# Two banks for the score matmuls of the maxima and three for those of the keys, instead of three and two

## The reference

```
x = x + attn_a(layernorm(x));  x = x + ffn(layernorm(x))
x = x + attn_b(layernorm(x));  x = x + ffn(layernorm(x))
attn:  softmax(q k^T / 4) v, per head, then a projection       (attn_b: causal, rotated q and k)
ffn:   gate = sigmoid(x Wq^T routers^T); leaf_prob = products of g or 1-g along 8 levels (256 leaves)
       leaf_prob @ leaf_values, then a projection
```

## Time and profile before

| | us |
|---|---|
| median of three runs (1170.36 to 1172.85) | 1172.26 |
| the profiled execution, its own time | 1170.09 |
| its span, from the first to the last instruction | 1168.4 |

### The profile page before, as it was taken

The page is one execution under the profiler, slowest core; times in us unless marked ns, Lnnn a source line. Parts: engine busy times, 40 slices in busy tenths (PEclk is TensorE's granted clock), DMA queues, the critical chain, the costliest instruction groups (busy, mean ns, idle before and its releaser), DMA issues.

```text
span 1168.4 us, 18914 instructions
## 1 busy us (share of the span) xinstructions
PE 1085.8 (93%) x6160; PEld 544.6 (47%) x6160; DVE 894.7 (77%) x2494; ACT 752.7 (64%) x1549; POOL 307.6 (26%) x339
## 2 busy tenths in 40 slices
PE   5789999999999999999999999999999899998986
PEld 2223354444455545454455544455444455544544
DVE  3578788786977988788976979788886878877834
ACT  3067766766777667765787567775776665666562
POOL 3012101111403151131503233041513526262210
PEclk9589999999999999999999999999999998999989
DMA  7323130600406023051314213150321313022001
GB/s 206 79 73 73 46 83 19 144 19 20 126 19 145 20 65 100 19 127 37 107 39 110 55 38 109 37 127 19 94 70 37 109 38 117 28 83 64 20 19 36
DMA packets 77921, 81.09 MB, mean 69 GB/s; under 512 B 12640, under 2 KB 65280, under 8 KB 77824
## 3 DMA queue, kind: packets, MB, share of 16 engines
q1 hardware_dynamic: 77760, 79.86, 25.5%
q0 software_dynamic: 64, 0.03, 0.0%
HBM read 20.84 MB, written 8.39 MB: 25 GB/s over the span
## 4 chain that ended last, share of the span: by engine, by line
PE 64%; DVE 21%; ACT 5%; issue 3%; SPq 3%; DMA 2%; POOL 2%; DVEq 0%; POOLq 0%; ACTq 0%
PE ps_work L1232 14%; PE ps_out L1141 13%; PE ps_max L1095 12%; PE ps_key L1117 11%; PE ps_work L1260 9%; DVE neg_max L859 7%; PE ps_work L1197 3%; DVE scratch L1009 3%; ACT probs L743 2%; DVE scratch L1012 2%; DVE ps_max L855 2%; DVE scratch L1039 2%; PE ps_work L1151 1%; SPq L500 1%; DMA q_stack<-q_part 1%
## 5 line engine op out<-in xcount | busy, mean ns | idle before, releaser
L743 ACT ACTIVATE probs<-ps_key 128x512 f32<-128x512 f32 (+3 forms) x1024 | 515.8, 520 | 340.9 <-PE ps_key L1117 336.0
L859 DVE TENSOR_REDUCE neg_max<-ps_max 128x1 bf16<-128x512 f32 x512 | 336.6, 685 | 87.0 <-PE ps_max L1095 85.6
L1095 PE MATMUL ps_max<-k_stack,q_stack 96*128 96x512 bf16 (+3 forms) x1024 | 355.9, 352 | 34.8 <-DVE neg_max L859 15.2
L1117 PE MATMUL ps_key<-q_stack,k_stack 97*128 97x512 bf16 (+3 forms) x1024 | 348.7, 344 | 19.2 <-ACT probs L743 13.1
L855 DVE CUSTOM_DVE_ANT_0 ps_max<-ps_max,mask_b 128x128 f32<-128x128 f32 (+3 forms) x512 | 247.0, 503 | 105.0 <-PE ps_max L1095 103.0
L1095 PEld LDWEIGHTS ps_max<-k_stack,q_stack 96*128 96x128 bf16 x1024 | 99.6, 97 | 292.7 <-DVE neg_max L859 115.0
L1141 PE MATMUL ps_out<-probs,v_ones 128*32 128x512 f32 (+3 forms) x2048 | 233.8, 529 | 0.6 <-POOL probs L638 0.6
L638 POOL TENSOR_SCALAR_AFFINE_SELECT probs<-probs 128x512 f32<-128x512 f32 x128 | 82.2, 643 | 400.5 <-ACT probs L743 400.0
L1117 PEld LDWEIGHTS ps_key<-q_stack,k_stack 97*128 97x128 bf16 x1024 | 100.9, 99 | 144.1 <-ACT probs L743 90.7
L1141 PEld LDWEIGHTS ps_out<-probs,v_ones 128*32 128x32 f32 x2048 | 40.4, 108 | 73.6 <-issue 63.2
L855 DVE DVE_READ_ACCUMULATOR2_ANT neg_max<- 128x1 bf16 x512 | 72.6, 142 | 0.0
(11 more groups left out here) (90 smaller groups left out, 1257.0 us busy)
## 6 DMA issues: line engine op xcount, KB each, us to landing
k_stack<-k_part SPq DMA_DIRECT2D x48, 256.0 KB
q_stack<-q_part SPq DMA_DIRECT2D x48, 256.0 KB
k_stack<-k_part SPq DMA_DIRECT2D x96, 128.0 KB
q_stack<-q_part SPq DMA_DIRECT2D x96, 128.0 KB
x_in<-in_x SPq DMA_DIRECT2D x8, 512.0 KB, 4.0
q_stack<-shift_rows SPq DMA_DIRECT2D x256, 1.0 KB, 1.7
x_again<-in_x SPq DMA_DIRECT2D x8, 512.0 KB, 4.1
spill<-x_plain SPq DMA_DIRECT2D x8, 512.0 KB, 2.9
```

The lines of the kernel that those rows point to most:

```text
L743: act.activation(probs[step % RING][:, j, q0:T], ps_key[slot % 2][:, 0:T - q0], ACT.Exp, scale=SCALE).then_inc(on["exp_done"], 1)
L859: dve.tensor_reduce(out=dst, in_=src, axis=AX_X, op=ALU.max, negate=True)\
L1095: pe.matmul(dst[:, 0:keys], q_stack[n % 2][0:SPLIT_ROWS, h, P * qt:P * qt + P], k_stack[n % 2][0:SPLIT_ROWS, h, 0:keys], start=True, stop= ...
L1117: pe.matmul(ps_key[slot % 2][:, 0:T - q0], k_stack[n % 2][0:STACK_ROWS, h, P * kb:P * kb + P], q_stack[n % 2][0:STACK_ROWS, h, q0:T], star ...
```

## The change

The number of score banks goes from three to two, that of key banks from two to three. A unit's bank is now its number, counted through all phases, modulo two, so a score matmul always waits for the maximum two units back. A slot's key bank is its number, counted through all phases, modulo three, on TensorE and on ScalarE, and a key matmul waits for the exponential three slots back.

```diff
-SCORE_BANKS = 3
+SCORE_BANKS = 2
+KEY_BANKS = 3
 def score_bank(n, unit):
-    return (unit + n % 2) % SCORE_BANKS
+    return (n * SLOTS + unit) % SCORE_BANKS
         ps_max = [bank(f"ps_max{i}", [P, T]) for i in range(SCORE_BANKS)]
-        ps_key = [bank(f"ps_key{i}", [P, T]) for i in range(2)]
+        ps_key = [bank(f"ps_key{i}", [P, T]) for i in range(KEY_BANKS)]
...
                 act.wait_ge(on["keyed_full"], count.next("keyed_full"))
-                act.activation(probs[step % RING][:, j, q0:T], ps_key[slot % 2][:, 0:T - q0], ACT.Exp,
+                act.activation(probs[step % RING][:, j, q0:T], ps_key[(n * SLOTS + slot) % KEY_BANKS][:, 0:T - q0], ACT.Exp,
                                scale=SCALE).then_inc(on["exp_done"], 1)
...
-                if count.some("exp_done", 1):
-                    pe.wait_ge(on["exp_done"], count.of("exp_done", 1))
+                if count.some("exp_done", KEY_BANKS - 1):
+                    pe.wait_ge(on["exp_done"], count.of("exp_done", KEY_BANKS - 1))
                 count.add("exp_done")
                 h = GROUP * g + j
-                pe.matmul(ps_key[slot % 2][:, 0:T - q0], k_stack[n % 2][0:STACK_ROWS, h, P * kb:P * kb + P],
+                pe.matmul(ps_key[(n * SLOTS + slot) % KEY_BANKS][:, 0:T - q0], k_stack[n % 2][0:STACK_ROWS, h, P * kb:P * kb + P],
                           q_stack[n % 2][0:STACK_ROWS, h, q0:T], start=True, stop=True).then_inc(on["keyed_full"], 1)
```

## The result

The changed kernel takes 1223.3 us (median of four runs, 1216.0 to 1227.7) against 1172.6 before: 1.0425 times as long, 95% interval 1.0401 to 1.0449 (the two medians alone give 1.043). Forecast were 1203 us, with a range to 1217. The direction was right, the size was not: 51 us and not 31.

What follows compares the result with a forecast made beforehand. TensorE's own work was taken to set most of the time, then VectorE's maxima. Score-bank losses of 34.3 us less 3.3 gained by the key bank gave 31.0 us, so 1203 us, 2.6% slower, range 1184 to 1217.

Steps and rivals of the forecast that it cites:

- The step that VectorE's queue runs dry and TensorE's lumps come out behind: Units 7 to 16 and 43 to 58 of each phase: two banks hold TensorE one unit earlier; 3.5 us per plain phase.
- the busy times of all engines should stay: All engines, whole run: no instruction, transfer or engine changes, so busy times stay and the other edits cost nothing.
- four plain phases (5, 7, 9, 11): Plain phases between causal ones: 1.1 + 0.9 + 1.5 = 3.5 us late each, 14.0 us together.
- four causal ones (4, 6, 8, 10): Causal phases between plain ones: shorter maxima, 0.9 and 0.8 us late in two places, 1.7 each, 6.8 together.
- phases 12 to 14: Last three full phases, causal with extra VectorE rotations: 0.9 and 2.0 us late, 2.9 each, 8.6 together.
- phases 2 and 3: Third phase +0.3 us after its key matmuls give 0.8 back; fourth phase, plain, 3.3 us.
- phase 15 and the end: The last phase was put at 1.3 us longer.
- phases 0 and 1: First two phases: third key bank removes 3.9 us in 6 waits and some 0.9; VectorE costs 1.5 back: -3.3 us.
- the opening loop: Opening, only score matmuls and maxima: two banks lose nothing, 0.48 us per refill against 0.60 us per maximum.
- the 0.06 and 0.42 us: Opening estimate: 0.06 us from a maximum's end to the waiting score matmul, 0.42 us more until its maximum can start.
- Buffering doesn't matter: Rival, TensorE's waits for VectorE: a bank only moves the waiting, only the key side counts; -13.1 us, 1159; chance 0.05.
- The delays add up: Rival, score-side delays: no give-back by idle time, +44 us or more, 1216 to 1225; chance 0.14 (over 1212).

Runs made afterwards that it cites:

- the run with long fills: Changed kernel plus two to four 512-column matmuls ahead of score matmuls of units 9, 11, 12, 13 (plain phases) and 10, 11, 12 (causal); 1200.1 us.
- fills in both places: Changed kernel plus added matmuls ahead of units 9 to 13 and, in phases with VectorE's rotations, of units 44, 51 and 52; 1201.9 us, ratio 1.0258.
- the kernel with two key banks: Changed kernel with two key banks as before and two score banks, one PSUM bank left unused; 1219.3 us, ratio to before 1.0403.
- the later values: Kernel before the change, with the second half of the values due two slots later, 48 instead of 46; 1174.2 us.
- the new numbering: Kernel before the change, with only the score banks' numbering made to run through all phases; 1175.3 us.
- the opening's fills: Kernel before the change, plus one 512-column matmul ahead of each of 19 opening score matmuls and twelve ahead of the first key matmul; 1174.1 us.
- the same short fills: Changed kernel with matmuls added ahead of score matmuls of units 9 to 13, cut from 512 columns to 8; 1213.3 us, ratio 1.0359.

## Why the prediction was wrong

The waits for the bank. The step that VectorE's queue runs dry and TensorE's lumps come out behind was right, in its places and, for the phases between, nearly in size. In phase 5 unit 13 was 1.74 late (read: 1.80), unit 44 another 1.24 (read: 1.25), and unit 52 another 1.70 (read: 1.70), here after the change:

```profile
449.40 0.39 PE L1096 MATMUL ps_max<-k_stack,q_stack 96*128 96x512 bf16 x1 [1.07 <-DVE neg_max L860]
...
460.26 0.39 PE L1096 MATMUL ps_max<-k_stack,q_stack 96*128 96x512 bf16 x1 [1.54 <-DVE neg_max L860]
```

At full clock (the run with long fills) a plain phase lost 2.9 us, not 3.5, a causal one 1.5, not 1.7: a little more was given back than I took.

The step that failed is the sentence that no engine's durations change ("the busy times of all engines should stay"). The sum held TensorE's durations at full clock while it put 34 us of new waits in front of TensorE (the trace shows 46 us more idle time), most of it in clusters ahead of a stretch in which TensorE is the bound. Half clock rose from 47.7 to 122.0 us after the first score matmul. In phases 1 to 14 that is 23 of the 46 us lost.

Two other terms failed as well. These are the terms of the sum, by the lengths of phases in the profiled executions, in us longer than before; the last column is the run with fills in both places, which was at full clock in phases 1 to 14:

| | forecast | changed kernel | its half clock, more than before | fills in both places |
|---|---|---|---|---|
| four plain phases (5, 7, 9, 11) | 14.0 | 22.9 | 27.3 | 12.1 |
| four causal ones (4, 6, 8, 10) | 6.8 | 10.4 | 10.2 | 5.8 |
| phases 12 to 14 | 8.6 | 4.8 | 10.2 | 0.5 |
| phases 2 and 3 | 3.6 | 7.3 | 10.2 | 4.1 |
| phase 15 and the end | 1.3 | 4.5 | 10.2 | 7.0 |
| phases 0 and 1 | -3.3 | 3.9 | 6.1 | 4.4 |

The column of half clock is a length, not what it costs. The lead-in differs by -0.7. What phase 15 and the end lost was not taken apart. That the run with fills came out at 1202, next to my 1203, is partly luck: its late phases are below the forecast, its first and last ones above it.

Phases 0 and 1: the opening loop is not free with two banks. The earlier trace rows had been taken with three banks, so it could not show that two satisfy it. And I had added the 0.06 and 0.42 us of stretches at full clock for a stretch in which the clock is at half (38.5 to 65.8 us before, 37.0 to 71.2 after). There a score matmul takes 0.61 us and not 0.39, so its maximum can start some 0.22 later, and 0.06 + 0.42 + 0.22 = 0.70 is more than the 0.60 of a maximum. After the change the timeline of the opening shows maxima at 9.06 for 13, one each 0.70 us (0.61 and 0.79 in turn), where the earlier trace rows has 0.60:

```profile
42.77 9.06 DVE L860 TENSOR_REDUCE neg_max<-ps_max 128x1 bf16<-128x512 f32 x13
...
43.52 1.21 PE L1096 MATMUL ps_max<-k_stack,q_stack 96*128 96x512 bf16 x2 [0.19 <-DVE neg_max L860]
```

The first key matmul came 1.1 us later for it. Then unit 24 waited 2.4 us, the catching up ran at half clock for 5 us longer (to 71.2 instead of 65.8), and slot 8's key matmul was 3.7 us late. From there the third key bank did give nearly what I had read: the waits of 0.8, 0.9, 0.7 and 0.9 us are gone, the lag was down to 2.0 us at slot 25, and the kernel with two key banks was 2.7 us behind there. The gain was there and the price ahead of it was missing. Six profiled executions with two score and three key banks have 66.1 to 66.7 us in phase 0, five with three score banks 62.6 to 63.0, and one, with the later values, 65.6, with 3.4 us more of half clock at 91 us, long after the opening; so the price is not the luck of one execution.

Phases 12 to 14 were over-estimated (with the clock kept they lost 0.5 us and not 8.6, against a kernel before that had 6.8 us of half clock there), since part of the delay was taken back. Before, TensorE stood at two phase boundaries for the copies of the next queries, 2.2 us at this one and 1.2 at a later one; the row is from the kernel before, from 926 to 931 us:

```profile
PE ps_max L1095 <- DMA q_stack<-q_part: 2.2, 1, 2.2
```

After the change phase 12 is 4.6 us late at its unit 63, but 2.0 at the next phase's first unit: the copies are done when TensorE comes. I had looked for idle time inside the phase and not at its end.

The rivals. "Buffering doesn't matter" had the right test, whether VectorE is still without idle time where TensorE's lump ends, and fell by it: behind unit 14 of phase 5 VectorE had run dry (the maximum at 415.71 above, where the earlier trace rows has eight in one go; at full clock, in the run with long fills, it was 0.16 us), and before maxima of plain phases it stood idle for score matmuls 112.2 us in all, against 85.6 before. "The delays add up" (1216 to 1225) hit the time for a reason that it didn't name: at full clock the waits did not add up, they were 23 us in phases 1 to 14, and it was the clock that filled the gap. A range that reaches its number by another mechanism is no sign that the mechanism holds.

## What to carry to other kernels

Where a change makes a nearly full TensorE wait in short clusters, price the clock beside the wait: take the stretch behind each cluster, see whether TensorE is the bound there, and count its durations at half clock too; here that doubled the loss in phases 1 to 14. Here a spare bank was worth most where the consumer works in bursts and the producer in lumps, and its worth is read from the distance of each matmul to the read that would newly gate it. When durations of a loop are added, take them from a row at the clock of that loop.

## What the runs showed of the hardware that I had not expected

With idle times of 0.70, 0.82, 0.75 and 0.95 us ahead of four units, and matmuls between them, TensorE's clock fell to half in each of four plain phases, for 6.8 us each. The kernel before, with 0.37, 0.82, 0.28 and 0.55 us in the same place, kept it in all four; but three more profiled executions with three score banks (the new numbering, the later values, the opening's fills), whose idle times ahead of units 11 to 13 are 0.37 to 0.42, 0.82 and 0.28 us, lost it in four of twelve plain phases, for 3.4 us each. So the fall was more frequent and longer with more idle time, and less of it did not exclude it.

Whether it falls varies also within one execution: the same short fills kept it in phase 7 and not in phase 5. The time follows it from run to run: of the four runs of the changed kernel the one of 1216.0 us had a mean granted clock of 0.959, those of 1223.1 and 1223.4 us 0.948, that of 1227.7 us 0.944.
